# First batch's shift and scale from a product onto 128 partitions, fills behind its norms, own queue entries for three batches, and the plan inside the MLP

## What is computed

```python
mod = (silu(c) @ wmod).reshape(16, 6, 1, 256)          # c: 16 x 256, wmod: 256 x 1536
sa, ca, ga, sb, cb, gb = (mod[:, i] for i in range(6))
ga, gb = (sign(g) * max(|g|, 0.25) for g in (ga, gb))
h = layernorm(x) * (1 + ca) + sa                       # x: 16 x 512 x 256
x = x + ga * mixer(h)
h = layernorm(x) * (1 + cb) + sb
x = x + gb * experts(h)                                # gate: top 2 of 8 experts per token

def mixer(x):
    xn = layernorm(x, g1, b1)
    attn = windowed_attention(xn)                      # 16 heads of 16, window 64 and the one before
    u, g = split(xn @ W_ug + b_ug); drive = xn @ B_w + u
    y = scan(s = A * s + drive) @ C_w
    x = x + sigmoid(g) * attn + (1 - sigmoid(g)) * y
    return x + gelu(layernorm(x, g2, b2) @ W1 + b1) @ W2 + b2
```

## Time and profile before

| | us |
|---|---|
| Median of three runs | 1973.43 (1969.89 to 1995.28) |
| Time of the profiled execution | 1956.55 |
| Its span | 1954.8 |
| PE busy | 1747.3 (89%) |
| DVE busy | 1411.5 (72%) |
| ACT busy | 999.3 (51%) |
| POOL busy | 1076.2 (55%) |

### The profile page before, as it was taken

How to read it: one execution, slowest core, us unless ns; L and a number is a source line. 1 busy time by engine, 2 the same in 40 slices (tenths; PEclk the granted TensorE clock), 3 DMA queues, 4 the chain that set the end, 5 groups by cost and what they waited for, 6 DMA issues and landing times. The chain is left out here.

```text
span 1954.8 us, 66166 instructions
## 1 busy us (share of the span) xinstructions
PE 1747.3 (89%) x23596; PEld 1356.7 (69%) x23597; DVE 1411.5 (72%) x3235; ACT 999.3 (51%) x1810; POOL 1076.2 (55%) x1304
## 2 busy tenths in 40 slices
PE   3899999999999999699999999409999999999997
PEld 1667777777777777566666666308888888888886
DVE  5788888888888887568988888715665665666665
ACT  2344444445444444356665555306665565565564
POOL 5333433333333333346888888634666666666664
PEclk6999999999999999899999999759999999999998
DMA  4232222223322222145455544313554545554553
GB/s 148 63 89 73 73 73 73 81 76 76 79 77 80 73 73 67 39 141 157 143 153 156 145 133 129 89 49 79 98 87 92 94 88 92 93 89 92 92 92 55
DMA packets 165884, 183.32 MB, mean 94 GB/s; under 512 B 37188, under 2 KB 146439, under 8 KB 165568
## 3 DMA queue, kind: packets, MB, share of 16 engines
q1 hardware_dynamic: 111488, 105.30, 19.7%
q0 software_dynamic: 36352, 56.78, 15.7%
q10 hardware_dynamic: 17856, 18.37, 2.7%
HBM read 109.40 MB, written 62.38 MB: 88 GB/s over the span
## 5 line engine op out<-in xcount | busy, mean ns | idle before, releaser
L1964 POOL DMA_INDIRECT out<-experts_y,experts_entry x144 | 236.8, 1645 | 191.2 <-DVE experts_y L1940 164.0
L1905 DVE TENSOR_SCALAR experts_v<-experts_v 128x512 f32<-128x512 f32 x144 | 73.7, 512 | 219.4 <-ACT experts_v L1879 219.4
L844 ACT ACTIVATE mixer_prob<-mixer_sc 128x1024 f32<-128x1024 f32 x128 | 131.4, 1026 | 165.0 <-PE mixer_sc L689 165.0
L1879 ACT ACTIVATE experts_g<-experts_pg,x_b 128x256 f32<-128x256 f32 x288 | 121.0, 471 | 182.9 <-PE experts_pv L131 182.8
L1954 POOL DMA_INDIRECT experts_rows<-scratch_xs,experts_entry x144 | 168.9, 1173 | 59.8 <-issue 43.3
L1579 POOL DMA_INDIRECT scratch_queue<-mlp_entry,mlp_slot x128 | 156.9, 1226 | 51.8 <-issue 36.1
L975 DVE TENSOR_REDUCE w_mx<-mixer_sc 128x8 bf16<-128x1024 f32 x128 | 156.3, 1221 | 24.3 <-PE mixer_sc L663 24.3
L129 PE MATMUL experts_pg<-experts_xT,x_w 128*128 128x256 f16 x576 | 158.1, 275 | 9.9 <-issue 7.0
L129 PE MATMUL experts_py<-x_w,experts_hh 128*128 x576 | 157.0, 273 | 2.0 <-DVE experts_hl L1917 2.0
L130 PE MATMUL experts_pg<-experts_xT,x_w 128*128 128x256 f16 x576 | 157.6, 274 | 0.0
L131 PE MATMUL experts_pg<-experts_xT,x_w 128*128 128x256 f16 x576 | 157.6, 274 | 0.0
(11 more groups left out here) (376 smaller groups left out, 5774.7 us busy)
## 6 DMA issues: line engine op xcount, KB each, us to landing
mixer_x<-in_x SPq DMA_DIRECT2D x64, 128.0 KB, 3.7
w_Kz<-mixer_Kt SPq DMA_DIRECT2D x64, 128.0 KB, 2.7
mixer_hres<-mixer_h SPq DMA_DIRECT2D x16, 512.0 KB, 4.5
scratch_xs<-scratch_mod SPq DMA_DIRECT2D x64, 128.0 KB, 3.5
scratch_x<-w_x SPq DMA_DIRECT2D x16, 512.0 KB, 2.8
scratch_n<-w_x SPq DMA_DIRECT2D x32, 256.0 KB, 2.3
w_nrm<-scratch_n SPq DMA_DIRECT2D x16, 512.0 KB, 5.3
mlp_stage<-in_x_w SPq DMA_DIRECT2D x16, 512.0 KB, 4.0
```

The lines of the kernel that those rows point to most:

```text
L844: act.activation(prob[:, n % 2, :].rearrange("p (c j) -> p c j", c=2), sc[:, 2:4, :], ACT.Exp, scale=SCALE).then_inc(exped.sem, 1)
L1879: act.activation(dst[:, q, f * ROWS:(f + 1) * ROWS], bank[:, q, f * ROWS:(f + 1) * ROWS], fn, bias=x["b1"][:, bass.ds(e, 1), bias + 2 * q ...
L1905: dve.tensor_scalar(v[:, q, :], v[:, q, :], -8.0, 10.0, ALU.max, ALU.min).then_inc(v_cut.sem, 1)
L1964: pool.indirect_dma_start(out=out, out_offset=bass.IndirectOffsetOnAxis(ap=entry[:, s, t, 0:1].bitcast(I32), axis=0), in_=y[:, s % 2, t, : ...
```

## The change

- A fourth bank, `row0`: TensorE multiplies, ahead of the three products, the first third of `wmod` with the column of batch 0 repeated 128 times. Shift and scale of batch 0 then stand in PSUM on all partitions, and DVE reads them there. The store and load by DRAM remain for batch 1 and later.
- SP loads the first tile of x in two halves, waits after the weights for the first norm, and loads batch 1 and the copies of the constants; then it stores shift and scale. Two new waits in batch 0: SP for `Kz`'s fill, ACT for `V`'s.
- POOL fills `Kz`, splits the bias rows and fills `V` after the second norm (`spaces`), and then makes the blanks.
- DVE: low parts 0 to 2 and the copies of the modulation go behind the second norm, `other_modulation` between `split_x` and `low_keys`, low parts 3 to 5 and `negate` ahead of the normalising of batch 1.
- MLP: `entry` and `slot` have four copies; the loop uses copy 0, the last three batches 1, 2 and 3, and only copy 0 waits for what was sent before. DVE chooses and places batch 14 before the scaling of batch 15; ScalarE and TensorE follow that order. The biases are loaded in the third batch, and their addition stands at the end. `plan` becomes a class, its constants made at the MLP's start, its 16 operations done behind the last `place`.
- The blocks `plan` and `expert_weights` fall away for 16 batches.

```diff
@@ -256,6 +258,11 @@
         pe.wait_ge(self.c_made.sem, 3)
+        pe.wait_ge(self.mod_in[0].sem, 16)
+        for k in range(KD):
+            last = pe.matmul(self.row0, self.sc[:, k, 0:1].to_broadcast([P, P]), self.wmod[:, k, 0:512],
+                             start=(k == 0), stop=(k == KD - 1))
+        last.then_inc(self.mod_mm.sem, 1)
         for n in range(3):
@@ -271,7 +278,7 @@
     def copy_modulation(self, dve, n):
-        dve.wait_ge(self.mod_mm.sem, n + 1)
+        dve.wait_ge(self.mod_mm.sem, n + 2)
         dve.tensor_copy(self.mod[:, n * 512:(n + 1) * 512], self.pm[n][0:self.NB, :]).then_inc(self.mod_sb.sem, 1)
...
             step(pool.memset(self.w[name][:, :, 0:WIN], 0.0))
-        step(pool.memset(self.w["Kz"][:].bitcast(F32), 0.0))
         step(pool.memset(self.w["mx"][:], 0.0))
...
             step(pool.memset(self.w["halfone"][:, a, DH * a:DH * a + DH], 1.0))
-        step(pool.memset(self.w["V"][:], 0.0))
         pool.sem_inc(self.made.sem, 1)
+
+    def spaces(self, pool):
+        pool.memset(self.w["Kz"][:].bitcast(F32), 0.0).then_inc(self.made.sem, 1)
+        self.split_rows(pool)
+        pool.memset(self.w["V"][:], 0.0).then_inc(self.made.sem, 1)
     def blanks(self, pool):
@@ -529,6 +535,8 @@
             def body(b, more):
+                if isinstance(b, int) and b == 0:
+                    sp.wait_ge(start.made.sem, 3)
                 sp.wait_ge(k_lo.sem, k_lo.at(b, 2))
@@ -563,18 +571,20 @@
                              x1[:]).then_inc(x1_out.sem, 16)
-            load_x(0)
+            for part in (slice(0, P // 2), slice(P // 2, P)):
+                sp.dma_start(x[part, 0, :], din["x"][0, part, :]).then_inc(x_in.sem, 16)
+            for t in range(1, TT):
+                load_tile(0, t)
             start.load_job(sp, 0)
...
                 start.load_job(sp, j)
+            sp.wait_ge(s_norm0.sem, 4)
+            load_x(1)
+            start.copy_constants(sp)
             start.store_shift_and_scale(sp)
             sp.wait_ge(start.mod_out.sem, 16)
-            load_modulation(0)
-            sp.wait_ge(s_norm0.sem, 4)
-            sp.wait_ge(s_h.sem, 2)
-            load(1)
-            start.copy_constants(sp)
+            load_modulation(1)
             body(0, True)
@@ -831,6 +841,8 @@
                 act.activation(drv[:], drive_bank, ACT.Identity, bias=w["bu"][:, 0:1]).then_inc(drive_sb.sem, 1)
+                if isinstance(b, int) and b == 0:
+                    act.wait_ge(start.made.sem, 4)
                 for u in range(4):
@@ -963,20 +975,18 @@
                                                  op0=ALU.mult, op1=ALU.subtract).then_inc(q_lo.sem, 1)
+                if isinstance(b, int) and b == 0:
+                    for j in range(3, 6):
+                        start.low_part(dve, j, start.low)
+                    start.negate(dve)
                 if not last:
...
                 for s in steps:
-                    if isinstance(b, int) and b == 0 and s == 0:
-                        for j in range(3, 6):
-                            start.low_part(dve, j, start.low)
-                        start.negate(dve)
                     if s < NW:
...
                                           AX.X, ALU.max).then_inc(maxed.sem, 1)
-                    if isinstance(b, int) and b == 0 and s == 3:
-                        start.other_modulation(dve)
                     if 0 <= s - 3 < NW:
@@ -1033,33 +1043,36 @@
             start.silu(dve)
-            dve.wait_ge(x_in.sem, 16 * TT)
+            dve.wait_ge(x_in.sem, 16 * TT + 16)
             moments(dve, 0, x, range(TT))
...
             normalize_first(x, s_norm0)
-            start.first_modulation(dve)
-            start.low_part(dve, 0, start.low)
-            start.low_part(dve, 1, start.low)
             start.add_drive(dve)
+            dve.wait_ge(start.mod_mm.sem, 1)
             dve.wait_ge(s_norm0.sem, 4)
-            dve.wait_ge(x_in.sem, 16 * TT + 16)
-            for n, (i, op) in enumerate(((1, ALU.mult), (0, ALU.add))):
-                src = nrm if i == 1 else h
-                for t in range(TT):
-                    dve.tensor_tensor(h[:, t, :], src[:, t, :], shsc[:, i, :], op).then_inc(h_first.sem, 1)
-                dve.wait_ge(h_first.sem, 4 * n + 4)
+            for t in range(TT):
+                dve.scalar_tensor_tensor(out=h[:, t, :], in0=start.row0[:, D:], scalar=1.0, in1=nrm[:, t, :],
+                                         op0=ALU.add, op1=ALU.mult).then_inc(h_first.sem, 1)
+            dve.wait_ge(h_first.sem, 4)
+            for t in range(TT):
+                dve.tensor_tensor(h[:, t, :], h[:, t, :], start.row0[:, 0:D], ALU.add).then_inc(h_first.sem, 1)
+            dve.wait_ge(h_first.sem, 8)
             moments(dve, 0, h, range(TT))
...
             normalize_first(h, s_norm1)
+            start.low_part(dve, 0, start.low)
+            start.low_part(dve, 1, start.low)
+            start.low_part(dve, 2, start.low)
             start.parity(dve)
-            start.low_part(dve, 2, start.low)
+            start.first_modulation(dve)
             start.copy_modulation(dve, 1)
...
             split_x(0)
+            start.other_modulation(dve)
             low_keys(0)
@@ -1109,7 +1122,8 @@
             start.constants(pool)
-            start.split_rows(pool)
+            pool.wait_ge(s_norm1.sem, 4)
+            start.spaces(pool)
             start.blanks(pool)
...
         slotf = m.sb("slotf", [P, TT * 2])
-        slot = m.sb("slot", [P, TT * 2], I32)
+        slot = m.sb("slot", [P, SENDS, TT * 2], I32)
         iota8 = m.sb("iota8", [P, E])
+        tiles = Plan(nc, ctx, keep, capacity, n_tiles(NB))
         pj = m.ps("pj", [P, 2, 512])
@@ -1242,6 +1258,10 @@
                     sp.dma_start(nrm[:], rows_of(scratch["n1"], b + 1)).then_inc(n1_in.sem, 16)
+                if behind == 2:
+                    sp.dma_start(x_w["b1"][:], din["x_b1"]).then_inc(bias_in.sem, 16)
+                    sp.dma_start(x_w["b2"][:], din["x_b2"].rearrange("(a e) d -> a e d", a=1).to_broadcast([P, E, D])
+                                 ).then_inc(bias_in.sem, 16)
                 sp.wait_ge(piece_lo.sem, piece_lo.at(b, 0))
@@ -1406,9 +1425,9 @@
             store_x2(NB - 1)
+            weigh(NB - 2)
             store_rows(NB - 1)
             copy_rows(NB - 1)
-            weigh(NB - 2)
             weigh(NB - 1)
@@ -1483,12 +1502,13 @@
                 return n
-            def place(a):
+            def place(a, q=0):
                 n = 13
-                dve.wait_ge(sent.sem, sent.at(a, 0))
+                if q == 0:
+                    dve.wait_ge(sent.sem, sent.at(a, 0))
                 dve.wait_ge(counted.sem, counted.at(a, 0))
-                dve.tensor_copy(entry[:, :, :, 0].bitcast(I32), ids[:].unsqueeze(2).to_broadcast([P, TT, 2])
+                dve.tensor_copy(entry[:, q, :, :, 0].bitcast(I32), ids[:].unsqueeze(2).to_broadcast([P, TT, 2])
                                 ).then_inc(counted.sem, 1)
@@ -1558,28 +1578,32 @@
             loop(dve, body)
-            place(NB - 3)
+            place(NB - 3, 1)
             moments_x2(NB - 1)
+            choose(NB - 2)
             dve.wait_ge(s_h2.sem, s_h2.at(NB - 1, 0))
             deviations(NB)
+            place(NB - 2, 2)
             scale_x2(NB - 1)
...
             split_rows(NB - 1)
-            for a in (NB - 2, NB - 1):
-                choose(a)
-                place(a)
+            dve.wait_ge(bias_in.sem, 32)
+            dve.tensor_scalar(x_w["b1"][:, :, FC:], x_w["b1"][:, :, FC:], 1.0, None, ALU.add).then_inc(bias_up.sem, 1)
+            choose(NB - 1)
+            place(NB - 1, 3)
+            tiles.make(dve)
         @block.gpsimd
         def _(pool):
-            def send(a):
+            def send(a, q=0):
                 wait_alone(pool, counted.sem, counted.at(a, 1), pool_passed)
...
                             out=scratch["queue"], out_offset=bass.IndirectOffsetOnAxis(
-                                ap=slot[:, 2 * t + k:2 * t + k + 1], axis=0),
-                            in_=entry[:, t, k, :], in_offset=None
+                                ap=slot[:, q, 2 * t + k:2 * t + k + 1], axis=0),
+                            in_=entry[:, q, t, k, :], in_offset=None
                         ).then_inc(sent.sem, 16)
...
                       allow_small_or_imprecise_dtypes=True).then_inc(ready.sem, 1)
+            tiles.constants(pool)
             loop(pool, body)
-            for a in (NB - 3, NB - 2, NB - 1):
-                send(a)
+            for q, a in enumerate((NB - 3, NB - 2, NB - 1)):
+                send(a, q + 1)
             pool.wait_ge(sent.sem, 16 * 2 * TT * NB)
@@ -2045,8 +2061,8 @@
             mlp(nc, din, w, x, scratch, out, NB, keep, capacity)
-            plan(nc, keep, capacity, n_tiles(NB))
-            expert_weights(nc, din, x, NB)
+            if NB < 2 * E:
+                expert_weights(nc, din, x, NB)
```

121 lines of the change are left out of this document (56 added, 65 removed).

## The result

| | before | after |
|---|---|---|
| Median, us | 1974.85 (1969.89 to 1995.28, four runs) | 1951.12 (1943.56 to 1965.45, four runs) |
| Profiled execution, us | 1956.55 | 1965.45 |
| Its span | 1954.8 | 1963.7 |

The ratio is 0.9886, with a 95% interval of 0.984 to 0.9932. The kernel is 1.1% faster where 1.85% was forecast, and the median lies 2 us above the range. The profiled execution of the new kernel is longer than the old one's, though the median is shorter. That has to be explained before any stage can be compared.

A forecast was written before the change was run, and what follows sets the result against it. TensorE fills the middle but idles or is held up at the start, batch 0 and the MLP-expert seam. Start-up 13.8 plus seam 22.5 gave 36.3 us off 1956.55, ratio 0.981, so a median of 1937 us, range 1918 to 1949.

The forecast's parts named there:

- sum of 36.3 us: Whole kernel: start-up 13.8 us plus seam 22.5 us saved; bounds 28.4 and 40.3.
- Up to N: Start, to the second norm's end: N at 25.3 instead of 36.7, 11.4 us earlier; bounds 11.0 and 11.9.
- From N to the first maximum: Batch 0, behind the second norm: moved work gives 2.0 us back; bounds a gain of 0.6, a loss of 5.5.
- Rival A: Start: POOL's fills hold DVE, 5.5 us given back, 31.4 us gained in all, 1942 us; chance 0.2.
- Batch 0, fourth step: Mixer, fourth to sixth maximum: nine modulation operations leave, 11.1 us becomes 6.6, a gain of 4.4, at least 3.0.
- Start-up: Start and batch 0 of the mixer together: 11.4 - 2.0 + 4.4 = 13.8 us gained.
- Seam, the sends: MLP's end: POOL starts the last eight sends at 1271.3 instead of 1281.87, 10.0 us gained; bounds 7.9 and 10.6.
- Rival B: Seam: the sends bind POOL, 7.9 us gained for 10.0, 34.2 in all, 1939 us; chance 0.12.
- Seam, plan and blocks: Between last sends and experts: plan and biases covered, SP goes on at once, 12.5 us gained; bounds 12.0 and 12.8.
- Rival D: Start-up: batch 0 gives all its gain back, only the seam's 22.5 us remain, 1951 us; chance 0.06.
- The sign for the last eight sends: Seam, new trace: the forecast is wrong if the last eight sends start later than 1260.
- I am wrong if [...] an MLP batch gets another length: MLP, new trace: a changed batch length would show the forecast wrong; no size given.

The follow-up runs named there:

- mod_back: Changed kernel with the gates' nine operations back at step 3 of batch 0; first maximum at 48.42 us for 52.05, one execution.
- fills_back: Changed kernel with both large fills (Kz and V) back among the constants, ahead of the first norm; first maximum at 50.30 us for 52.05, one execution.
- after_again: The changed kernel run once more, unchanged; 1961.11 us, 0.987 to the kernel before.
- after_spread: Changed kernel, MLP loop sending five pieces together and one behind each of the first three tiles' sums; 1932.10 us, 0.9707 to the kernel before.
- seam_only: Kernel before with only the seam part of the change (own queue entries, plan and biases in the MLP); 1963.14 us, 0.9893 to the kernel before.
- start_only: Kernel before with only the start-up part of the change; 1977.13 us, 0.9959 to the kernel before.
- before_spread: Kernel before, MLP loop sending five pieces together and one behind each of the first three tiles' sums; 1959.23 us, 0.9844 to the kernel before.
- spread_b: Changed kernel with fills on ScalarE, first x in four loads, five sends together, one behind each of three tiles' sums; 1923.78 us, 0.9758 to the kernel before.
- spread_a: Changed kernel with ScalarE fills, first x in four loads, four sends together, four behind three tiles' sums; 1962.06 us, 0.9953 to the kernel before.

## Why the prediction was wrong, point by point

In short: the sum of 36.3 us had its terms at the right places, and two of them were too large. The way from the second norm (N) to the first maximum gave back 5.0 us for 2.0, because nine small operations were priced alone and ran beside POOL's fill. The last sends came 7.3 us earlier for 10.0, because hand-overs read where POOL was silent were moved to where it sends. And the mixer's loop lost 1.8 us, which the sum had at nothing. On top of that the MLP was taken to have one length, and it has two.

**Up to N: right.** N came at 25.16, 11.6 us earlier; 25.3 and 11.4 were forecast. The multiply and the add from PSUM took 1.41 each, where I took 1.5 (16.22 and 17.67 are their starts). The x load in five pieces cost 1.04 us (statistics at 9.82 for 8.78), where I had said under 0.5; the first norm still ended at 15.97 for 15.6, as it was not held up.

**From N to the first maximum: the mis-sized term.** 2.0 us back were forecast, it was 5.0. The failed step is "The rest of the modulation, nine small operations [...], lies in the 3.5 us in which DVE waited for the keys". The pause was there, 3.6 us by `mod_back`'s row and by the keys' 35.03, but the nine operations took 9.6 us. Of these 2.7 are L287's wait for the V fill, 1.5 L292's beside the bias rows' subtraction, and the rest the other holds and the 3.1 us that they take alone. Without the V fill (`fills_back`) the way from N to the first maximum is 2.4 us shorter; without the nine operations in it (`mod_back`) 3.6. The place of the bottleneck was wrong too: I had POOL's list late, free at N + 17.1, but POOL was free at 41.0, N + 15.8, and waited 3.86 us for DVE's seeds. Rival A had the mechanism (the fills hold DVE) and its price, 5.5, but was argued away because the longest operations of that list have two inputs. That was true of the weights' low parts (1.22 us beside the Kz fill), and not of L947 beside POOL's subtraction and cast (2.17 us for two, 1.29 before); the ones held most were the short ones with one input. By the Trainium skill, page "SBUF — State Buffer", section "Who interferes with whom", copies, casts and `tensor_scalar` are among the operations that can take the shared pair; L287 (2.95 for 0.28) and L293 (1.54 for 0.27) agree.

**Batch 0, fourth step: right.** 6.57 us from the fourth to the sixth maximum for 6.6 forecast, 4.5 us gained for 4.4. But it was bought: by `mod_back` the same nine operations cost 3.6 us in front of the first maximum. The move as a whole is worth at most 1.5 us, by the sixth maximum (69.37 in `mod_back`, 68.49 and 67.90 in the changed kernel) and by batch 1's keys.

**What the sum did not have.** TensorE's waits in the code of batch 0 (1.11 and 1.68 us) and the half clock behind a pause. They are in some executions and not in others. Another 1.8 us goes between batch 1's keys (11.3 gained) and the MLP's beginning (9.5): from the keys of batch 1 to those of the last batch it takes 667.2 to 668.8 us with the old start and 668.6 to 670.7 with the new, 0.1 us for each batch of the loop. Why is open. Start-up: 9.5 for 13.8.

**Seam, the sends: mis-sized.** 7.3 us for 10.0 (33.3 to 26.0 from first send to first send; three profiles of the kernel before, and `after`, `after_again`, `after_spread` and `seam_only`; `start_only`, with the old seam, has 34.2). The rows of batch 15 were split 13.4 us after the first send, as worked out (13.8). What failed is the step from "Turning and gate products took from 1257.7 to 1261.6, 3.9" straight to the choosing, which puts the hand-over to DVE at nothing, and the hand-over in "placing and hand-over 2.5". The products themselves kept their 3.9. In the old trace POOL was silent at both places, since it waited for the entries (no send between 1258.55 and 1264.68, nor between 1277.1 and 1281.87). In the new one it sends beside them, and from the split rows to the logits' copy it took 5.7 us, from the placing to the send 3.7. With the sends away they take 3.95 and 2.4. Rival B had nearly this price, 7.9, for another reason: the sends did not bind. They kept their 1.26 us, and POOL idled 2.10 us before the last eight.

**Seam, plan and blocks: right.** From the last eight sends to the first gather 12.3 us less, 12.5 forecast (29.7 to 17.4, the same profiles).

**The ratio and the median.** The sum of 36.3 us was to be 27 to 30: 27.1 between the two spread kernels, 28.5 from the stages. A gain of 27.1 in 1959 is a factor of 0.9862, which on 1973.43 gives 1946 us. The other 5 us of the measured median are not accounted for run by run: 0.9862 lies inside the interval of the measured ratio (0.984 to 0.9932), and how many long batches the single runs of either kernel had is known only for the profiled ones. Long batches are the likeliest part, since one more of them in a run is 3 us. I took a profile with none of them as the base, and treated the MLP as a stage that the diff does not touch and that therefore has one length. "I am wrong if [...] an MLP batch gets another length" was the right alarm, but the row split's spacing could not have told of it from one profile. What could have been seen is that the median lay 0.9% above the profiled execution, and runs up to 2%: 38.7 us between the two, which is 12.5 batches of 3.1 us. Rival D's 1951 us is the measured median by chance: the start-up kept 9.5 us. The sign for the last eight sends, not later than 1260, failed too: they started at 1301.4, some 33 us of it from long batches.

**A version that beats both** is `after_spread`, 0.9707 to before and 27 us under `before_spread`. `spread_b` has 0.9758 beside another run of the kernel before, on another chip; they were not run side by side, so whether ScalarE's fills add to it is open.

## What to carry to other kernels

A duration read where another engine was silent can't be moved to where that engine works: look who is idle beside the row. Small operations put into a pause fit only if they are priced with the neighbour that will run there; try to move that neighbour first. When the runs of a kernel spread by more than the effect sought, look for the stage with two lengths and take it out of both kernels before comparing them.

## What the runs showed of the hardware

While GpSimd issued a train of indirect sends, other engines went on 1.3 to 4.9 us after the work that they waited for had ended: 0.2 us from the last gate product to its reader without sends, 1.9 to 2.9 with them; DVE's first sum 3.5 to 3.6 us behind the second product's start in short batches, 7.7 in long ones. With one or four sends to a batch a batch took 25.0 us, with five in a train and three single ones 26.0 to 26.5, with six and two 27.5, with eight in a train 26.1 or 29.2 by execution. Which path the signals share with the sends is not shown, nor why the same kernel has short batches in one execution and long ones in another; `spread_a` shows only that four sends and four single ones don't help when the last one is waited for. ScalarE filled 2048 words to a partition in 1.89 us, and VectorE's operations beside it kept their times (1.41 us for an add of four tiles, as without it); GpSimd took 3.51 us for 4096 and held VectorE's L287 until it ended.
